# Second attention of a gated cross-attention kernel: row normalisation on GpSimd, all exponentials on ScalarE with a negated maximum as bias, two transposes later on TensorE

## The reference

```python
x = x + tanh(g_xattn[1]) * L1_xattn(layernorm(x), ctx, ...)
x = x + tanh(g_ffn[1])   * L1_ffn(layernorm(x), ...)
# L1_xattn: 16 heads of width 8
scores = einsum('bhqd,bhkd->bhqk', q, k) * scale + rel_bias   # 128 x 77 per head
attn   = softmax(scores, axis=-1)
out    = einsum('bhqk,bhkd->bhqd', attn, v) @ Wo + bo
# L1_ffn: idx = argmax(x @ sign(tile_sigs).T); row uses W[idx], b[idx]
```

## Time and profile before

| | us |
|---|---|
| median of 3 runs | 525.89 (523.97 to 528.09) |
| the profiled execution | 527.66 |
| its span, first to last instruction | 525.9 |
| TensorE busy | 476.1 (91%) |
| VectorE busy | 387.8 (74%) |
| GpSimd busy | 346.6 (66%) |
| ScalarE busy | 300.7 (57%) |

### The profile page before, as it was taken

One profiled execution on the slowest core, in us unless ns is written; L12 is line 12 of the kernel. 1 busy time (PEld: TensorE's weight loads), 2 busy tenths in 40 slices (PEclk: granted clock), 3 DMA queues, 4 the chain that ended last, 5 costly groups with the idle time before them and its releaser, 6 DMA issues.

```text
span 525.9 us, 12375 instructions
## 1 busy us (share of the span) xinstructions
PE 476.1 (91%) x3378; PEld 301.8 (57%) x3378; DVE 387.8 (74%) x1178; ACT 300.7 (57%) x981; POOL 346.6 (66%) x813
## 2 busy tenths in 40 slices
PE   6957986599998999879999999999999999999993
PEld 5956865455655666646555555555555555655441
DVE  2889998567333333346899999999999999999852
ACT  3756574312254555248767766776767667676630
POOL 5565677777045545445788787878888777878532
PEclk9999897589999999958999999999999999999997
DMA  8875530031144222100000000000000000000000
GB/s 228 169 116 149 160 89 17 26 79 60 31 106 123 79 70 69 41 16 7 11 11 22 12 21 22 12 22 11 22 12 21 12 22 15 18 16 7 12 6 16
DMA packets 33923, 25.77 MB, mean 49 GB/s; under 512 B 8104, under 2 KB 31280, under 8 KB 33824
## 3 DMA queue, kind: packets, MB, share of 16 engines
q1 hardware_dynamic: 30864, 19.48, 15.0%
q0 software_dynamic: 2272, 4.67, 2.8%
q10 hardware_dynamic: 720, 0.83, 0.7%
HBM read 16.89 MB, written 8.39 MB: 48 GB/s over the span
## 4 chain that ended last, share of the span: by engine, by line
PE 48%; DVE 2%; issue 1%; POOL 1%; POOLq 0%; ACT 0%; DVEq 0%
PE bank L1362 13%; PE bank L1311 8%; PE bank L1297 8%; PE bank L1287 6%; PE bank L1378 2%; PE bank L1348 2%; PE bank L1283 1%; PE bank L1344 1%; PE bank L1332 1%; PE bank L1328 1%; PE bank L1323 1%; PE bank L1273 1%; PE bank L1367 1%; PE bank L1269 1%; PE bank L1384 1%
## 5 line engine op out<-in xcount | busy, mean ns | idle before, releaser
L1425 ACT ACTIVATE wgu<-wgu,top 128x77 f32<-128x77 f32 x256 | 67.4, 347 | 15.7 <-DVE top L1527 15.7
L1362 PE MATMUL bank<-w,xn3T 128*128 128x512 f32 x128 | 71.7, 644 | 0.1
L1435 ACT ACTIVATE PRT<-bank 128x512 f32<-128x512 f32 (+1 forms) x128 | 54.5, 426 | 28.7 <-PE bank L1297 28.1
L969 POOL DMA_INDIRECT routed<-ys,to x39 | 37.4, 960 | 48.6 <-DVE ys L1172 40.6
L1297 PE MATMUL bank<-cst,wgu 128*128 128x128 f32 x320 | 60.2, 287 | 0.6 <-DVE wgu L1534 0.3
L1517 DVE TENSOR_TENSOR wgu<-bank,biasQ 128x616 f32<-128x616 f32 x64 | 50.9, 795 | 8.3 <-PE bank L1287 7.0
L1311 PE MATMUL bank<-PRT,VP 128*32 128x128 f32 x1024 | 54.5, 285 | 0.7 <-ACT PRT L1435 0.7
L1527 DVE TENSOR_REDUCE top<-wgu 128x8 f32<-128x616 f32 x64 | 50.3, 786 | 1.1
L1287 PE MATMUL bank<-KB,QT 32*128 32x308 f32 x256 | 50.2, 433 | 0.0
L1167 DVE TENSOR_TENSOR hid<-actg,bank 128x256 f32<-128x256 f32 x39 | 16.4, 422 | 41.1 <-ACT actg L1076 41.1
L1297 PEld LDWEIGHTS bank<-cst,wgu 128*128 128x128 f32 x320 | 37.8, 142 | 15.0 <-issue 13.2
(11 more groups left out here) (230 smaller groups left out, 1253.3 us busy)
## 6 DMA issues: line engine op xcount, KB each, us to landing
xs<-sorted_x SPq DMA_DIRECT2D x39, 64.5 KB, 1.8
wgu<-in_wgu SPq DMA_DIRECT2D x4, 512.0 KB
y<-routed SPq DMA_DIRECT2D x32, 64.0 KB, 1.8
out<-res SPq DMA_DIRECT2D x32, 64.0 KB, 1.7
ctxT<-in_ctxT SPq DMA_DIRECT2D x16, 77.0 KB, 3.4
mask<-in_mask SPq DMA_DIRECT2D x16, 77.0 KB, 3.6
wdn<-in_wdn SPq DMA_DIRECT2D x2, 512.0 KB
X<-in_x SPq DMA_DIRECT2D x1, 768.0 KB, 5.5
```

The lines of the kernel that those rows point to most:

```text
L969: nc.gpsimd.indirect_dma_start(routed, bass.IndirectOffsetOnAxis(ap=to[:, t:t + 1], axis=0), ys[t % WAYS][:, :], None).then_inc(st_y[t % W ...
L1362: nc.tensor.matmul(map_bank(b, k)[:, :], xn3T[u][:, :], w2[:, k * HT:(k + 1) * HT, :], start=True, stop=True).then_inc(s["f"], 1)
L1425: last = nc.scalar.activation(SC[u][:, head, :], SC[u][:, head, :], ACT.Exp, bias=top[u][:, head:head + 1])
L1435: nc.scalar.activation(PT[half][:, k], bP[end][:, 0:k.stop - k.start], ACT.Exp if half else ACT.Copy).then_inc(s["pTs"], 1)
```

## The change

GpSimd's `inv_std` becomes `normalise`: add eps, power, and then one tensor_scalar over the 128 columns that subtracts the mean and multiplies by the reciprocal deviation. ScalarE's `norm2` and `norm3` go. Both halves of the maxima are negated, `subtract` goes, and ScalarE makes the exponentials of the second half too, head by head with the maximum as bias, in two stages of four heads at two places of its list. The copies of the transposed blocks are plain copies for both halves. On TensorE the second half's transposes move behind `choice_T`, and the weighing stages of each half come together.

```diff
@@ pe_program, probs_T and the list @@
         def probs_T(n):
-                pe.wait_ge(s["su" if half else "ex"], b + 1)
+                pe.wait_ge(s["ex"], 3 * b + 2 * half + 1)
...
         pipeline(pe, B, [
-            (signature, 5), (weigh(0), 3), (probs_T(2), 3), (weigh(1), 3), (probs_T(3), 3), (choice_T, 5),
-            (project, 4), (weigh(2), 3), (maps(0), 5), (scores(1), 2), (weigh(3), 3), (maps(1), 5),
+            (signature, 5), (weigh(0), 3), (weigh(1), 3), (project, 4), (choice_T, 5), (probs_T(2), 3), (probs_T(3), 3),
+            (maps(0), 5), (scores(1), 2), (weigh(2), 3), (weigh(3), 3), (maps(1), 5),
             (shared("queries"), 0), (queries, 1), (shared("T0"), 0), (probs_T(0), 2), (heads_T, 3),
...
@@ act_program @@
-        def exps(h):
+        def exps(first, last):
             def stage(b, u):
-                act.wait_ge(s["lo"], 1 * b + h + 1)
-                for head in range(h * HH, (h + 1) * HH):
-                    last = nc.scalar.activation(SC[u][:, head, :], SC[u][:, head, :], ACT.Exp, bias=top[u][:, head:head + 1])
-                last.then_inc(s["ex"], 1)
+                act.wait_ge(s["lo"], 2 * b + first // HH + 1)
+                for head in range(first, last):
+                    done = nc.scalar.activation(SC[u][:, head, :], SC[u][:, head, :], ACT.Exp, bias=top[u][:, head:head + 1])
+                done.then_inc(s["ex"], 1)
...
-                nc.scalar.activation(PT[half][:, k], bP[end][:, 0:k.stop - k.start], ACT.Exp if half else ACT.Copy).then_inc(s["pTs"], 1)
+                nc.scalar.activation(PT[half][:, k], bP[end][:, 0:k.stop - k.start], ACT.Copy).then_inc(s["pTs"], 1)
...
-            (shared("pe0"), 0), (probs_T(0), 2), (shared("norm2"), 0), (norm2, 0), (norm3_T, 4),
-            (probs_T(1), 2), (mixed_T, 3), (shared("xTs"), 0), (norm_T, 0), (probs_T(2), 2), (choice_T, 4),
-            (probs_T(3), 2), (exps(0), 1), (heads, 2), (shared("qs"), 0), (queries, 0), (norm3, 3)])
+            (shared("pe0"), 0), (probs_T(0), 2), (exps(HH, HH + HG), 2), (norm3_T, 4), (shared("norm2"), 0),
+            (probs_T(1), 2), (mixed_T, 3), (shared("xTs"), 0), (norm_T, 0), (exps(HH + HG, NH), 2), (choice_T, 4),
+            (probs_T(2), 2), (probs_T(3), 2), (exps(0, HH), 1), (heads, 2), (shared("qs"), 0), (queries, 0)])
...
@@ dve_program @@
         def maxima(h):
-                nc.vector.tensor_reduce(top[u][:, k], SC[u][:, k, :], AX.X, ALU.max, negate=(h == 0)).then_inc(s["mx" if h else "lo"], 1)
+                nc.vector.tensor_reduce(top[u][:, k], SC[u][:, k, :], AX.X, ALU.max, negate=True).then_inc(s["lo"], 1)
-        def subtract(h):
...
-            (add_bias, 5), (shared("mix"), 0), (mix, 3), (shared("sub1"), 0), (subtract(1), 2)], drain=drain)
+            (add_bias, 5), (shared("mix"), 0), (mix, 3), (shared("sub1"), 0)], drain=drain)
...
@@ pool_program @@
-        def inv_std(x):
+        def normalise(x):
...
                 nc.gpsimd.tensor_tensor(ve[u][:, :], mv[u][:, 1:2], eps[:, :], ALU.add).then_inc(s[mid], 1)
-                nc.gpsimd.tensor_tensor(nm[u][:, :], mv[u][:, 0:1], minus[:, :], ALU.mult).then_inc(s[mid], 1)
...
                 nc.gpsimd.tensor_tensor(r[u][:, :], ve[u][:, :], power[:, 0:1], ALU.pow).then_inc(s[mid], 1)
-                nc.gpsimd.tensor_tensor(nb[u][:, :], nm[u][:, :], r[u][:, :], ALU.mult).then_inc(s[shift], 1)
+                nc.gpsimd.tensor_scalar(xn[u][:, :], rows[u][:, :], mv[u][:, 0:1], r[u][:, 0:1], ALU.subtract,
+                                        ALU.mult).then_inc(s[done], 1)
```

More of the change, by code:

```diff
@@ L1198, in attend_1 @@
     r2 = [sb(f"r2{u}", [128, 1]) for u in two]
-    nm2 = [sb(f"nm2{u}", [128, 1]) for u in two]
-    nb2 = [sb(f"nb2{u}", [128, 1]) for u in two]
     xn2 = [sb(f"xn2{u}", [128, D]) for u in two]
@@ L1387, in pe_program @@
         drain = {
-            B + 2: [(signature, 5), (weigh(0), 3), (probs_T(2), 3), (weigh(1), 3), (probs_T(3), 3), (project, 4),
-                    (choice_T, 5), (weigh(2), 3), (maps(0), 5), (weigh(3), 3), (maps(1), 5), (heads_T, 3),
+            B + 2: [(signature, 5), (weigh(0), 3), (weigh(1), 3), (project, 4), (choice_T, 5), (probs_T(2), 3),
+                    (probs_T(3), 3), (maps(0), 5), (weigh(2), 3), (weigh(3), 3), (maps(1), 5), (heads_T, 3),
                     (picked_bias, 5), (norm3_T, 4), (warm(3), 3), (mixed_T, 3)],
@@ L1434, in stage @@
                 k = slice(HG * S, BH * S) if end else slice(0, HG * S)
-                nc.scalar.activation(PT[half][:, k], bP[end][:, 0:k.stop - k.start], ACT.Exp if half else ACT.Copy).then_inc(s["pTs"], 1)
+                nc.scalar.activation(PT[half][:, k], bP[end][:, 0:k.stop - k.start], ACT.Copy).then_inc(s["pTs"], 1)
             return stage
[L1438 to L1442, removed]
-        def norm3(b, u):
-            act.wait_ge(s["nb3"], b + 1)
-            wait(act, s["zT"], b - 1)
-            nc.scalar.activation(xn3[u][:, :], x3[u][:, :], ACT.Identity, bias=nb3[u][:, 0:1],
-                                 scale=r3[u][:, 0:1]).then_inc(s["xn3"], 1)
         def heads(b, u):
@@ L1503, in stats2 @@
             dve.wait_ge(s["x2"], b + 1)
-            wait(dve, s["nb2"], b - 1)
+            wait(dve, s["xn2"], b - 1)
             nc.vector.bn_stats(st2[u][:, :], x2[u][:, :]).then_inc(s["st2"], 1)
@@ L1524, in stage @@
                 k = slice(h * HH, (h + 1) * HH)
-                if h == 0:
-                    wait(dve, s["ex"], b - 1)
-                nc.vector.tensor_reduce(top[u][:, k], SC[u][:, k, :], AX.X, ALU.max, negate=(h == 0)).then_inc(s["mx" if h else "lo"], 1)
-            return stage
-        def subtract(h):
-            def stage(b, u):
-                dve.wait_ge(s["mx"], b + 1)
-                k = slice(h * HH, (h + 1) * HH)
-                nc.vector.tensor_tensor(SC[u][:, k, :], SC[u][:, k, :],
-                                        top[u][:, k].rearrange("p (h o) -> p h o", o=1).to_broadcast([128, HH, SK]),
-                                        ALU.subtract).then_inc(s["su"], 1)
+                wait(dve, s["ex"], 3 * (b - 2) + 2 * h + 1)
+                nc.vector.tensor_reduce(top[u][:, k], SC[u][:, k, :], AX.X, ALU.max, negate=True).then_inc(s["lo"], 1)
             return stage
@@ L1552, in residual @@
             wait(dve, s["x3b"], b - 1)
-            wait(dve, s["nb3"], b - 1)
             wait(dve, s["xn3"], b - 1)
@@ L1642, in with_bias @@
             nc.gpsimd.tensor_tensor(x2b[u][:, :], x2[u][:, :], bo1[:, :], ALU.add).then_inc(s["x2b"], 1)
-        def inv_std(x):
-            mv, ve, nm, r, nb, ready, mid, shift, used = x
+        def normalise(x):
+            rows, mv, ve, r, xn, ready, mid, done, used = x
             def stage(b, u):
```

14 lines of the change are left out of this document (6 added, 8 removed).

## The result

| | before | changed |
|---|---|---|
| median (4 runs each) | 526.46 us | 535.58 us |
| ratio | | 1.0174 [1.014, 1.0208] |
| the profiled execution, its span | 527.66, 525.9 | 535.51, 533.7 |
| first row of `x2` to first `choose` | 31.65 | 35.66 |
| 28 turns | 237.32 | 240.37 |

The change costs 1.7%, 9.1 us between the medians. Between the two profiled executions 7.85 us lie: +4.0 in the ramp (first row of `x2` to first `choose`), +3.05 in the 28 steady turns, +0.95 in the drain (from the 29th `choose` on), -0.16 ahead of the phase. The forecast had +2.0, +2.1 and -0.4.

The account below looks back on a forecast made before the run. A ring of waits across engines, closed by ScalarE's copy, was taken as the bound. 28 x (8.53 - 8.456) = 2.1, ramp +2.0, drain -0.4 gave +3.7 us: 529.5, by itself 525 to 532.5, 8 in 10 within 523 to 542.

Parts of the forecast that it names:

- a dearer normalisation: Rival: GpSimd's normalisation costs over 0.46 us, delaying choose's last step by up to 0.18; ring to 8.71, 530 to 535; chance 0.17.
- The new link: Second maxima 0.78, hop 0.04, four ScalarE exponentials 1.00, then copy and 0.76 to choose; alone makes the ring 8.68 us.
- TensorE's walk: TensorE's path from the start of choose through transposes, scores and weighs to the second pick: 5.27 us.
- the ring: Per-item cycle from choose over pick, second maxima, exponentials and copy back to choose: 8.48 us, 8.55 with GpSimd's delay, 8.53 taken.
- The normalisation: GpSimd's 128x128 tensor_scalar, twice a turn: 0.46 us each, net +0.13 each, against 0.56 won.
- GpSimd under the choice: GpSimd's L1669 runs beside choose's last step on VectorE, which ends 0.02 after it, at 9.44: ring 8.55 us.
- The subtraction, L1663 at 0.73: Removing VectorE's 0.84 us subtraction gains nothing on the ring; GpSimd's L1663 falls from 1.29 to 0.73.
- Earlier rows: Normalised rows on GpSimd start after 0.90 and stand after 1.36 us, earlier than today, so off the path.
- The ramp: Turns before the steady stretch: ScalarE's exponentials make one 1.2 us longer, those beside it about 0.8; +2.0 (0.5 to 2.5).
- The drain: Final turns: two normalisations each lose a 0.2 us hop to ScalarE, -0.4 in all.
- Keys: Rival: GpSimd's L1612 starts before choose's last step, which waits 0.70 instead of taking 0.23; ring 8.95, 541.3 us; chance 0.20.
- TensorE the bound: Fast rival: four saved changes of matmul shape at about 0.1 each give 0.4 us a turn, 515 us; chance 0.10.

Follow-up runs that it names:

- the run with the filling: Changed kernel with choose's masked ranks in PSUM, plus eleven TensorE matmuls nobody reads in the ramp turn of item 0's first weighing: 523.52 us, ratio 0.9983.
- the kernel with the ranks in PSUM: Changed kernel with the masked ranks of choose in a free corner of its PSUM bank instead of SBUF: 526.72 us, ratio 1.0001.

## Why the prediction was right, and where not

Forecast 529.5, range 523 to 542, measured 535.58: in the range, above the 525 to 532.5 of the likeliest case. The rival "a dearer normalisation" (530 to 535) is the one that came, in the steady turns; by time it does not reach the result either, for the ramp was mis-sized. The range held the result, the sum did not: 3.7 was forecast, 7.85 lie between the profiled executions. Of the 4.15 too little, 0.95 stand in the turns and 3.35 in ramp and drain, where TensorE's granted clock fell, a term that the forecast had left out. That the total lies in the range is in part luck: the steady turns alone were near, and one of two errors in them hid the other.

- *The new link* was right: exponentials behind the second maxima, then the copy, 1.03 idle ahead of `choose`. From pick to `choose` 3.19 pass, 3.21 was taken.
- *TensorE's walk*: pick at 5.27 forecast, about 5.13 without the hold (8.32 - 3.19). The second weigh costs 0.22 (0.58 for the pair against 0.36), not 0.29, and the scores 1.02, not 1.06. So the ring itself is 8.32, not 8.48, a gain of 0.13 on 8.456.
- *The normalisation* was mis-sized: 0.80 taken twice, where 0.46 was taken and 0.73 was the upper bound. The nearest row by columns (a tensor_tensor of 128) misled; the true price is above the row with twice the columns. The rival for it counted each 0.01 once, but the normalisation stands twice in GpSimd's list. The estimate from the Trainium skill's page "GPSIMD Engine Reference", section "Performance versus the Vector engine", 0.38, was further off.
- *GpSimd under the choice* is the step of the turn that failed. I had L1669 end 0.02 before the choice and "up to 0.18" for a dearer normalisation, and I let GpSimd begin the second normalisation 0.08 after its statistics, as if the first one's price did not matter; it begins 0.40 after. Twice 0.34 put GpSimd so much later that not the last sum but the middle one, L1638, lies on L1547 and holds it for 0.26. A hold is not a slope: what counts is which instruction covers the step. Ring 8.59 against 8.53 taken; two errors of opposite sign, -0.16 in the ring and +0.22 in the hold.
- *The subtraction, L1663 at 0.73*: right. *Earlier rows*: they start after 0.94 (forecast 0.90) but stand after 1.74, not 1.36. The reading of the kernel before was off too: ScalarE starts on them 1.45 after GpSimd's first step in most turns, not 1.18, and they stand after 1.93. With the later first step the rows now stand 0.13 later behind their statistics (2.14 against 2.01), not earlier. TensorE does not wait for them in the steady turns, so they are off the path as said.
- *The ramp*: +4.0 for +2.0, outside the bounds. The turn named (5.90 long before) grew by 1.27, 1.2 was forecast; the turns beside it, costed at 0.8, by 3.98, of which, by the run with the filling, the clock is the larger part. What failed here is the overlap: the extra work on ScalarE was costed as its own time, not as idle time of TensorE, behind which the clock fell. The two growths make 5.25; 1.24 came back between the first row and the second scaling of queries (12.63 for 13.87), which is not the change's: the kernel before with its ranks in PSUM alone shows 12.59 there.
- *The drain*: +0.95 for -0.4. Its loss is one turn at the lower clock, 9.07; in the kernel with the ranks in PSUM, with the same waits of 0.17, 0.54 and 0.22 on TensorE ahead of it, that turn is 7.64 and the drain 32.99. The other traces with the paired order show either value too, and 9.19 came without the rest of the change. So this loss is not shown to be the change's, and why the clock fell in one and not in the other stays open. The 32.99 is 0.45 under the one before, the -0.4 forecast, but by luck: the normalisation alone on GpSimd leaves the drain at 33.44, and the paired order without it has 32.70.
- *Keys* did not come here, but it did with the normalisation back on ScalarE. *GpSimd the bound* and *TensorE the bound* did not come. But TensorE's order was worth 0.33 a turn, near the 0.4 that the fast rival spoke of: what the change gained on TensorE it gave to the link (0.20) and the hold (0.27).

## What to carry to other kernels

Before moving work to an idle engine, look at what stands behind it in that engine's list: here ScalarE had over 2 us free in a turn, and four exponentials in front of one copy, with the hold that TensorE's better order uncovered, cost more than that order gave. Try the parts of a change apart; the order with the ranks in PSUM was 1.9% faster, without them 0.9%, the whole 1.7% slower. And where an engine may hold another, ask which instruction will lie on the short step, and whether its source can be put where no hold is possible.

## What was not expected of the hardware

- A GpSimd tensor_scalar with two per-row operands over 128x128 takes 0.80 us, a tensor_tensor of the same size 0.46 and one of twice the size 0.73.
- A step of eight columns on VectorE takes 0.23, 0.49 or 0.75 by which GpSimd instruction runs beside it, and 0.23 always with its source in PSUM. It was free beside an instruction that started 0.12 behind it, and held by one that started 0.02 behind it.
- The same waits on TensorE went with a granted clock of 1.00 in some turns and 0.83 in others: 8.82 or 10.25 a turn. Filling an idle stretch in one place did not keep the clock up in another, nor in the same place in every execution.
